# Degrees, row normalisation and table scaling of a GNN layer as one stage, with split node one-hots

## What is computed

```python
xn  = layernorm(x)                                     # per row, no affine part
deg = segment_sum(edge_weight ++ ones, row ++ self)    # weighted degree and self loop
dinv = where(deg > 0, rsqrt(deg), 0)
norm = dinv[row] * edge_weight * dinv[col]
h7  = segment_sum((xn @ W)[col] * norm[:, None], row) + b
x   = x + gcn_mlp(h7) + mix(xn)                        # mix(xn) also adds xn itself
x   = x + moe(layernorm(x))
```

## Time and profile before

| | us |
|---|---|
| median of three runs | 4658.87 |
| profiled execution | 4660.25 |
| its span | 4658.5 |
| records in, turned and cut (802.7 to 837.6) | 34.9 |
| batches (837.6 to 1074.5) | 236.9 |
| degrees to dinv, and the first scalings (1074.5 to 1082.0) | 7.5 |
| table written (1082.0 to 1166.0) | 84.0 |
| gather and mix (1166.0 to 3655) | 2489 |

### The profile page before, as it was taken

The page is one execution under the profiler, slowest core; times in us unless marked ns, Lnnn a source line. Parts: engine busy times, 40 slices in busy tenths (PEclk is TensorE's granted clock), DMA queues, the critical chain, the costliest instruction groups (busy, mean ns, idle before and its releaser), DMA issues. The chain is left out here.

```text
span 4658.5 us, 80245 instructions
## 1 busy us (share of the span) xinstructions
PE 3532.4 (76%) x20196; PEld 2666.5 (57%) x20196; DVE 3032.5 (65%) x7684; ACT 1516.5 (33%) x4675; POOL 2709.1 (58%) x2419
## 2 busy tenths in 40 slices
PE   7777775791677777877765778777777679999986
PEld 6445543570344444444443666665666469999885
DVE  8899997883555655655554555555555675555566
ACT  2455553663111111111100322222222255555442
POOL 0488887000666666666666666666666325555553
PEclk9677787555888887888877888888898789999998
DMA  2111112454333333333333444444445712222456
GB/s 73 3 3 3 3 3 36 133 166 142 110 110 109 109 108 110 112 109 110 111 102 92 132 133 131 127 132 130 133 132 124 155 37 71 67 69 69 142 198 220
DMA packets 297683, 472.63 MB, mean 101 GB/s; under 512 B 97283, under 2 KB 195850, under 8 KB 297615
## 3 DMA queue, kind: packets, MB, share of 16 engines
q0 software_dynamic: 140544, 273.69, 23.8%
q1 hardware_dynamic: 149919, 194.17, 12.4%
q10 hardware_dynamic: 7154, 3.99, 0.3%
HBM read 350.37 MB, written 123.70 MB: 102 GB/s over the span
## 5 line engine op out<-in xcount | busy, mean ns | idle before, releaser
L1483 POOL DMA_INDIRECT rows<-table,idx x1664 | 1688.0, 1014 | 799.1 <-issue 466.4
L1764 DVE TENSOR_TENSOR acc<-acc,ps_seg 128x256 f32 x1664 | 697.1, 419 | 939.0 <-remote 669.2
L1929 PE MATMUL ps_seg<-rows,pick 128*128 128x256 f32 x3328 | 955.4, 419 | 129.6 <-issue 63.6
L1929 PEld LDWEIGHTS ps_seg<-rows,pick 128*128 128x128 f32 x3328 | 654.7, 208 | 355.1 <-issue 241.8
L756 POOL DMA_INDIRECT records<-sort_rec,sort_addr x280 | 527.6, 1884 | 262.0 <-DVE sort_rec L859 159.4
L1608 DVE TENSOR_SCALAR pick<-iota_row,loc,ewt 128x128 f32<-128x128 f32 x1680 | 530.3, 362 | 3.9
L1801 PE MATMUL ps_kv<-wkv,xT 128*128 128x512 f32 x392 | 264.5, 811 | 246.5 <-ACT xT L1506 149.1
L2367 POOL DMA_INDIRECT y_rows<-arena,idx x212 | 256.1, 1208 | 293.8 <-DVE arena L2414 235.7
L2499 PE MATMUL ps_h<-arena,up_now 128*128 128x128 f32 x3392 | 420.6, 278 | 0.0
L2483 PE MATMUL ps_y<-down_now,arena 128*128 128x256 f32 x1696 | 402.7, 381 | 0.0
L2499 PEld LDWEIGHTS ps_h<-arena,up_now 128*128 128x128 f32 x3392 | 401.2, 194 | 1.8 <-issue 0.3
(11 more groups left out here) (380 smaller groups left out, 5372.9 us busy)
## 6 DMA issues: line engine op xcount, KB each, us to landing
rows<-table,idx POOLq DMA_INDIRECT x1664
acc<-y_rows SPq DMA_DIRECT2D x28, 640.0 KB
rows_x<-in_x SPq DMA_DIRECT2D x100, 128.0 KB
xn<-xn_dram SPq DMA_DIRECT2D x100, 128.0 KB
xn_dram<-acc SPq DMA_DIRECT2D x98, 128.0 KB
skip_dram<-rows_skip SPq DMA_DIRECT2D x98, 128.0 KB
table<-acc SPq DMA_DIRECT2D x98, 128.0 KB
xT_dram<-xT SPq DMA_DIRECT2D x98, 128.0 KB
```

The lines of the kernel that those rows point to most:

```text
L1483: pool.indirect_dma_start(out=rows[:, t, :], out_offset=None, in_=k.table, in_offset=bass.IndirectOffsetOnAxis(idx[:, h, t:t + 1], 0), bou ...
L1764: dve.tensor_tensor(here, here, sums(u), ALU.add).then_inc(added[u], 1)
L1929: pe.matmul(sums(t), pick[:, h, t, :], rows[:, t, :], start=True, stop=True).then_inc(summed_up[t], 1)
```

## The change

`degrees_and_rows` and `scale_table` become one function without a barrier between them and without a hardware loop; every trip is written out. The 1664 tiles are handled in 26 groups of 64. A node's place in its block is split into a high part of 4 and a low part of 32 values: VectorE writes a one-hot of 4 columns and one of 32 columns, multiplies the first by the three weight pieces to 12 columns, and TensorE multiplies 32-column weights by these 12 columns. Rows are normalised in 25 chunks of four blocks, 7 of them ahead of group 0, with one square root, one reciprocal and one shift for a chunk. GpSimd adds the skip rows from x and the normalised row. Weight pieces are cast on ScalarE, each into pairs. After every two groups (one trip j of 13) the degrees are summed, the inverse roots of the blocks that are complete (READY, 7 or 8 of them) are taken, their rows scaled by ScalarE and VectorE and written to the table. Chunks are written with one DMA for four blocks. The bias is cut at the start. The rows of x live in a ring of three chunks.

```diff
-                degrees_and_rows(k)
-                k.phase_done()
-                scale_table(k)
+                degrees_rows_table(k)
                 k.phase_done()
...
+    GROUP = P // 2
+    GROUPS_T = 2 * TRIPS
+    NORM = 4
+    NORMS = -(-BLOCKS // NORM)
+    LEAD = 7
+    EARLY = 2
+    X_CHUNKS = 3
+    HIGH, LOW = P // 32, 32
+    READY = [BLOCKS * P * j // TILES_USED for j in range(TRIPS)] + [BLOCKS]
...
+                def load(c):
+                    for u, at in enumerate(k.naturals(sp, NORM * c, len(blocks_of(c)))):
+                        sp.dma_start(x[:, c % X_CHUNKS, u:u + 1, :], x_blocks[:, bass.ds(at, 1), :]).then_inc(
+                            x_in[c % X_CHUNKS], 16)
+
+                def put(c):
+                    b = blocks_of(c)
+                    start_after(sp, xn_out[c % X_CHUNKS], 16 * (c // X_CHUNKS))
+                    sp.wait_ge(xn_done, b.stop)
+                    sp.dma_start(xn_blocks[:, b.start:b.stop, :], k.acc[:, b.start:b.stop, :]).then_inc(xn_out[c % X_CHUNKS], 16)
+                    sp.wait_ge(skip_done, b.stop)
+                    sp.dma_start(skip_blocks[:, b.start:b.stop, :], skip[:, c % 2, 0:len(b), :]).then_inc(skip_out[c % 2], 16)
+
+                def put_table(j):
+                    at = k.naturals(sp, READY[j], len(ready(j)))
+                    sp.wait_ge(act_scaled, act_total(j))
+                    sp.wait_ge(dve_scaled, dve_total(j))
+                    for u, n in enumerate(ready(j)):
+                        sp.dma_start(table_blocks[:, bass.ds(at[u], 1), :], k.acc[:, n:n + 1, :]).then_inc(table_out, 16)
...
+                for c in range(NORMS):
+                    put(c)
+                    if c + X_CHUNKS < NORMS:
+                        load(c + X_CHUNKS)
+                    g = c - LEAD
+                    if g >= 7 and g % 2 == 1:
+                        put_table(tabled)
+                        tabled += 1
+                for j in range(tabled, TRIPS):
+                    put_table(j)
...
+                def skipped(c):
+                    pool.wait_ge(x_in[c % X_CHUNKS], loads_of(c))
+                    start_after(pool, skip_out[c % 2], 16 * (c // 2))
+                    for u, n in enumerate(blocks_of(c)):
+                        pool.wait_ge(xn_done, n + 1)
+                        pool.tensor_tensor(skip[:, c % 2, u, :], x[:, c % X_CHUNKS, u, :], k.acc[:, n, :],
+                                           ALU.add).then_inc(skip_done, 1)
...
+                def one_hots(g):
+                    dve.tensor_tensor(
+                        at_high[:, :, :].rearrange("p t (a two) -> p t a two", two=2),
...
+                    start_after(dve, tile_summed, g - 1)
+                    dve.tensor_tensor(
+                        at_low[:, r, :, :].rearrange("p t (c two) -> p t c two", two=2),
...
+                    dve.wait_ge(high_done, g + 1)
+                    dve.tensor_tensor(
+                        weighted[:, r, :, :, :].rearrange("p t v (a two) -> p t v a two", two=2),
...
+                for g in range(GROUPS_T + 6):
+                    c = g + LEAD
+                    if c + 1 < NORMS:
+                        moments(c + 1)
+                    if g < GROUPS_T:
+                        one_hots(g)
+                    if 1 <= g <= GROUPS_T:
+                        keep(g - 1)
+                    if c < NORMS:
+                        inverses(c)
+                    if g >= 4 and g % 2 == 0 and (g - 4) // 2 < TRIPS:
+                        degrees((g - 4) // 2)
+                    if g >= 5 and g % 2 == 1 and (g - 5) // 2 < TRIPS:
+                        inverse_roots((g - 5) // 2)
+                    if g >= 6 and g % 2 == 0 and (g - 6) // 2 < TRIPS:
+                        scaled((g - 6) // 2)
+                    if g % 2 == 1 and g < GROUPS_T:
+                        blocks_of_tiles(g // 2)
...
+                        for t in range(GROUP):
+                            at = t % HALF_BANK * WIDE
+                            last = pe.matmul(ps_t[r][t // HALF_BANK][0:LOW, at:at + WIDE], at_low[:, r, t, :],
+                                             weighted[:, r, t, :, :].rearrange("p v a -> p (v a)"), start=True, stop=True)
                         last.then_inc(tile_summed, 1)
```

## The result

The kernel after takes 4551.9 us (median of four runs, 4547.44 to 4556.83) against 4657.65 us before (four runs): ratio 0.9773, 95% interval 0.9759 to 0.9786. The forecast was 4534 us in a range of 4508 to 4590. The saving is 105.8 us; 125 were forecast.

What follows compares the result with a forecast made beforehand. TensorE's loop matmuls, then SyncE's serial issues were taken to bound the old stage. The new one sums 62.3 + 126.0 + 33.6 + 13.5 + 2.7 = 238.1 for 363.4 us: 125.3 saved, 4534 us, range 4508 to 4590.

Steps and rivals of the forecast that it cites:

- opening: Stretch from the first record load to group 0's one-hots at 865.0: 62.3 us, against 34.9 before.
- 18 groups: Groups of 64 tiles with moments still to take: 7.0 us each, 126.0 us in all.
- last 8 groups: Groups without moments: VectorE's 3.9 us and some waits, 4.2 us each, 33.6 us in all.
- end and barrier: From the last matmuls through scalings, eight issues and landing, 13.5 us, then the barrier, 2.7 us.
- VectorE's 6.1 us: VectorE's work for a group with moments; the rival that it alone sets the pace: 4518 us, chance 0.04.
- the chain of release, write, load and landing: Row chunks' path through the ring of three, back to VectorE: 13.4 us for two groups, 6.7 each.
- first leg: From the end of a chunk's shift through normalisations, add, writes and loads to landing: 8.3 us.
- the rest, put at 5.05: VectorE's part of the two-group chain after landing: moments, one-hots, reductions and inverses, 5.05 us.
- this path (21.1 for three groups, 7.0 each): The chunk chain when it runs through a table put: 21.1 us for three groups, its next leg shorter.
- The queue rival: Loads land later than 2.4 us behind the writes in one queue: a group 8.5 us, 4561 us, chance 0.15.
- the sentence: TensorE paces the old loop of 104 batches: 144 ns a matmul, 2.3 us a batch of 16 tiles.
- The rival in which VectorE is held up: GpSimd's adds and VectorE's one-hots shut each other out: up to 69 us, to 4603 us; chance 0.17.

Runs made afterwards that it cites:

- the ring of five: The changed kernel with x rows in a ring of five chunks instead of three, skip rows added in place; ratio 0.9730 to the kernel before, stage 237.8 us.
- the inverses first: The changed kernel with a chunk's reciprocal, shift and normalisation moved to the start of a group's work; ratio 0.9731 to the kernel before, stage 242.3 us.
- three low one-hots: The changed kernel with the 32-column one-hot written three times in each group; 4307.92 us, stage 310.1 us.
- table at the end: The changed kernel with all table rows issued after the last block is scaled; 4319.72 us, stage 313.3 us.

## Why the prediction was right, and where it was off

The time lay in the range, 18 us above the forecast. By its steps, the stage measured against the sum:

| term | forecast | measured |
|---|---|---|
| opening | 62.3 | 72.3 |
| 18 groups | 126.0 (7.0 each) | 131.5 (7.3 each) |
| last 8 groups | 33.6 | 33.0 |
| end and barrier | 16.2 | 21.8 |
| stage | 238.1 | 258.5 |

**The groups.** The mechanism was right and is shown by the ring of five and by the inverses first: not VectorE's 6.1 us but the chain of release, write, load and landing. Its first leg, put at 8.3 us, measured 9.8 (from the end of chunk 7's shift at 876.1 to chunk 10's statistics at 885.9); the rest, put at 5.05, was 4.7. That gives 7.25 a group. The leg was longer because the data landed about 3 us behind the last issue instead of 2.4 (for which no row of before stood), and the register load, put at 0.44 for four values, mostly took 0.56 to 0.9. In the later groups the leg is 11.6 to 12.4 us, since writes and loads queue behind table rows. The prediction had this path (21.1 for three groups, 7.0 each) and set it aside because "its next leg is shorter"; groups 9 to 16 took 7.93 us and without the table rows 7.01. The queue rival (8.5 a group) was wrong in its size: with a longer ring the same queue carries 6.5. What it costs lies in the order of the issues more than in the landing.

**The opening** was the term that missed most, 10 us. Half of it is a turn that the sum left out. The loop's first turn takes the moments of chunk 8 ahead of group 0's one-hots, where the forecast let group 0 begin behind those of chunk 7:

```profile
867.29 1.41 DVE L1171 BATCH_NORM_STATS2 rows_stats<-rows_x 128x6 f32<-128x256 f32 x4 [2.09 <-DMA rows_x<-in_x]
868.61 0.36 DVE L1174 BATCH_NORM_AGGREGATE rows_mv<-rows_stats 128x2 f32<-128x6 f32 x4
872.33 1.41 DVE L1171 BATCH_NORM_STATS2 rows_stats<-rows_x 128x6 f32<-128x256 f32 x4 [3.36 <-DMA rows_x<-in_x]
873.65 0.36 DVE L1174 BATCH_NORM_AGGREGATE rows_mv<-rows_stats 128x2 f32<-128x6 f32 x4
873.93 0.26 DVE L1247 TENSOR_TENSOR rows_at_high<-rows_iota_b,rows_high 128x256 bf16<-128x256 bf16 x1
```

Chunk 7's moments end at 869.0 (forecast: 864), and chunk 8's wait and moments take 5.0 us more. Of the 5 us before that, the third weight piece ended at 849.2 instead of 847, and the rest lies in the waits for chunks 5 to 7. Two of the smaller causes are in this stretch of the timeline:

```profile
819.64 8.97 POOL L1084 TENSOR_TENSOR rows_skip<-rows_x,acc 128x256 f32<-128x256 f32 x8 [17.85 <-ACT acc L1103]
820.99 0.42 SPq L1045 DMA_DIRECT2D xn_dram<-acc  x1
821.67 3.61 DVE L1209 TENSOR_TENSOR acc<-acc 128x3328 f32<-128x3328 f32 x1
...
825.89 0.36 SPq L1047 DMA_DIRECT2D skip_dram<-rows_skip  x1
827.00 1.92 SPq L1038 DMA_DIRECT2D rows_x<-in_x  x4
```

Eight adds take 8.97 us. One of them lasts 4.18 us, from 821.7 to 825.9, while VectorE's join of the records runs beside it, and so chunk 0's skip rows leave at 825.9 and chunk 3 is asked for from 827.0 on. The join itself began 1.3 us later than put. The held-up add costs little in the end: with the skip rows on ScalarE the opening is 71.4 us. With the ring of five it is 63.7.

**The end.** SyncE needs 6.0 us per trip in the last three, not 4.6: their register loads of seven or eight values, put at 0.66, took 1.7 to 1.9. Its loads over the stage, those of four values among them (min/median/max ns):

```profile
L187 SPq TENSOR_LOAD <-perm x38: 301/750/2662, 803.0 to 1051.5; - x38
```

Of the 13 loads for table rows two took 0.71 us and the others 0.95 to 2.66. All begin 0.04 us behind a DMA issue, so that alone is not what makes them long, and the cause stays open. The last three trips are scaled within 6 us of each other, so three of these stand in a row at the end.

**TensorE** did pace the old loop, as the prediction said: between 860 and 1040 us it was busy for 173.4 of 180, and VectorE's one-hots waited for it 42 times. What the sentence left out is the worth of it: with matmuls at 37 ns the batches kept 2.27 of 2.33 us. The price of 37 ns in the new code was right in kind (29 measured, for 32 weight columns and 12 columns), and the sum did not need the sentence, as it replaced the whole stage. In the new order the loop would count for more: by an estimate 64 matmuls at 144 ns are 9.2 us a group, above the 7.3 measured. No run has the new groups in a hardware loop.

**GpSimd.** One add was put at 0.70 us and took 0.72 alone. The rival in which VectorE is held up is real in its mechanism and small in its price: of 52 scalings 24 met an add, and 17 of these took 0.81 to 0.90 us instead of 0.35; four low one-hots took 1.74 instead of 1.22. Put as high as 69 us, it was some 10 us of VectorE's time, in the shadow of the waits for rows. What the Trainium skill says in "SBUF — State Buffer", "Who interferes with whom", on instructions with two inputs agrees with the one-hots and with the add beside the 3.61 us join; the scalings, one tensor and a column of factors, are held up as well. What the Trainium skill says in "GPSIMD Engine Reference", "Engine selection", that elementwise work belongs on VectorE, was not tried: no run has the adds there. With them on ScalarE and on GpSimd the times are the same.

**The gather stage** was said to be paced by GpSimd's indirect loads. On another chip it took 2199 us instead of 2492, with the same 1688 us of GpSimd and a granted clock of 0.94 instead of 0.84:

```profile
1060.00:3259.00 2199.00, 1846.00 (x6966) 1190.75 (x6967) 1434.89 (x4550) 499.82 (x951) 1688.19 (x1669) 0.94 0.47 132
```

So it doesn't stand at GpSimd's pace alone. That TensorE's clock is what makes the difference is argued from this row, not tried. Nothing of the forecast hung on it.

**Where the 105 us came from.** The split one-hots are worth about 52 us (three low one-hots, an estimate of what they replace) and the table's writes beside the groups 55 (table at the end). Each was measured with the other in place. That the two come near the whole does not show that nothing else counts: the opening costs 37 us more than before, so other parts gave as much. Row chunks, fewer small instructions and the code without a loop were not taken out one by one in the new kernel. The skip rows on GpSimd have no part in it.

## To carry to other kernels

When three resources lie within some 12% of each other, the busy shares don't tell what removing the first is worth: go on to what the second costs per turn. A stage that has been made denser can next be held by the depth of its ring, from release to landing; here a larger ring gave 20 us of stage and an earlier release 15. Put the stage's serial queue (here 98 issues at 0.5 to 0.8 us) beside other work, and then look at what its issues stand in front of: here they lengthen the groups beside them by 0.8 to 0.9 us. Count the turns ahead of a loop from the code: one that was left out is half the miss of the opening.

## Not expected of the hardware

- A matmul in a hardware loop whose operands are computed in registers was issued every 133 to 144 ns; the same one in written-out code every 37 ns, at the same granted clock, 0.50 (1.2 GHz).
- A register load of seven or eight values on SyncE took 0.71 to 2.66 us right behind a DMA issue, most of them over 1.4, though one of a single value took 0.27 us there. Why is open.
- A GpSimd add of 256 columns took 4.18 us instead of 0.72 beside a VectorE add of 3328 columns, and a VectorE scaling of one tensor by a column mostly 0.81 to 0.90 instead of 0.35 us beside a GpSimd add. Statistics beside adds were not held up (0.41 us both ways).
